# A hybrid transformer block: value steps in pairs in TensorE's order of a group

## What is computed

```python
x = x + _L0_attn_a_ref(_layernorm(x, axis=-1), L0_attn_a_w_qkv, L0_attn_a_w_o)
x = x + _L0_ffn_ref(_layernorm(x, axis=-1), L0_ffn_kernel, L0_ffn_scale)
x = x + _L0_attn_b_ref(_layernorm(x, axis=-1), L0_attn_b_w_qkv, L0_attn_b_w_o)
x = x + _L0_ffn_ref(_layernorm(x, axis=-1), L0_ffn_kernel, L0_ffn_scale)
```

```python
scores = jnp.einsum('bhsd,bhtd->bhst', xq, keys) * scale
causal = jnp.tril(jnp.ones((seq, seq), dtype=bool))[None, None]
scores = jnp.where(causal, scores, -jnp.inf)
probs = jax.nn.softmax(scores, axis=-1)
out = jnp.einsum('bhst,bhtd->bhsd', probs, values)
```

## Time and profile before

| | |
|---|---|
| runs, us | 1556.15, 1555.02, 1553.38 (median 1555.02) |
| span of the profiled execution, us | 1552.2 |
| busy: TensorE, VectorE, ScalarE, GpSimd | 1439.5, 1132.0, 998.2, 413.6 us |
| idle before the exponentials (L793), waiting for scores (L571) | 261.0 us |
| idle before the reductions (L974), waiting for L551 | 186.7 us |
| idle before the matmuls of L571, L549, L589 | 10.5, 17.9, 6.3 us |

### The profile page before, as it was taken

How to read it: one execution, slowest core, us unless ns; L and a number is a source line. 1 busy time by engine, 2 the same in 40 slices (tenths; PEclk the granted TensorE clock), 3 DMA queues, 4 the chain that set the end, 5 groups by cost and what they waited for, 6 DMA issues and landing times.

```text
span 1552.2 us, 36760 instructions
## 1 busy us (share of the span) xinstructions
PE 1439.5 (93%) x10756; PEld 799.7 (52%) x10756; DVE 1132.0 (73%) x1620; ACT 998.2 (64%) x1800; POOL 413.6 (27%) x786
## 2 busy tenths in 40 slices
PE   5989999998798999999879899999988899999997
PEld 4844444446674444444667444444466744444455
DVE  6897777736788777773768877777377887777646
ACT  4967667663496667675349667766625966776652
POOL 3423222212242322221224222222123422222211
PEclk9999999999899999999989999999998999999999
DMA  3000000001000000000210000000010000000001
GB/s 112 2 29 3 1 1 1 1 1 42 3 1 29 2 1 1 1 1 1 83 69 1 29 3 1 1 1 1 2 41 3 1 30 2 1 1 1 1 21 75
DMA packets 11421, 23.26 MB, mean 15 GB/s; under 512 B 816, under 2 KB 2608, under 8 KB 11312
## 3 DMA queue, kind: packets, MB, share of 16 engines
q1 hardware_dynamic: 11312, 21.89, 4.0%
HBM read 16.91 MB, written 4.19 MB: 14 GB/s over the span
## 4 chain that ended last, share of the span: by engine, by line
PE 73%; DVE 11%; issue 8%; POOL 3%; ACT 3%; DMA 1%; DVEq 0%; POOLq 0%; ACTq 0%; SPq 0%
PE psE L571 17%; PE psO L589 17%; PE psM L549 14%; PE psM L483 13%; DVE mx L974 4%; PE psM L551 3%; PE psT L466 2%; PE psT L532 2%; PE psO L532 2%; ACT probs L793 1%; PE psT L559 1%; DVE stats L876 1%; PE psE L466 1%; PE psM L466 1%; DVE xn L896 1%
## 5 line engine op out<-in xcount | busy, mean ns | idle before, releaser
L974 DVE TENSOR_REDUCE mx<-psM 128x1 f32<-128x768 f32 (+6 forms) x704 | 697.2, 1023 | 189.7 <-PE psM L551 186.7
L793 ACT ACTIVATE probs<-psE 128x512 f32<-128x512 f32 (+1 forms) x1216 | 656.8, 574 | 272.3 <-PE psE L571 261.0
L571 PE MATMUL psE<-qT,kT 115*128 (+4 forms) x1536 | 415.7, 331 | 10.5 <-ACT probs L793 7.4
L549 PE MATMUL psM<-kT,qT 112*128 (+4 forms) x1536 | 376.4, 327 | 17.9 <-DVE mx L974 13.8
L1163 POOL TENSOR_SCALAR_AFFINE_SELECT probs<-probs 128x512 f32<-128x512 f32 x256 | 162.3, 636 | 660.7 <-ACT probs L793 659.9
L589 PE MATMUL psO<-probs,v_grp 128*32 128x512 f32 (+3 forms) x3072 | 323.0, 499 | 6.3 <-POOL probs L1163 3.8
L571 PEld LDWEIGHTS psE<-qT,kT 115*128 (+1 forms) x1536 | 126.2, 97 | 289.0 <-ACT probs L793 152.5
L551 PE MATMUL psM<-tri_b,ident_b 128*128 128x128 bf16 x1024 | 210.3, 220 | 0.0
L549 PEld LDWEIGHTS psM<-kT,qT 112*128 (+1 forms) x1536 | 139.4, 98 | 108.6 <-DVE mx L974 31.1
L551 PEld LDWEIGHTS psM<-tri_b,ident_b 128*128 128x128 bf16 x1024 | 99.7, 97 | 65.5 <-issue 0.6
L589 PEld LDWEIGHTS psO<-probs,v_grp 128*32 128x32 f32 x3072 | 63.3, 108 | 104.3 <-issue 66.7
(11 more groups left out here) (90 smaller groups left out, 1553.8 us busy)
## 6 DMA issues: line engine op xcount, KB each, us to landing
probs<-in_w_qkv SPq DMA_DIRECT2D x5, 1536.0 KB, 6.3
xs<-in_x SPq DMA_DIRECT2D x8, 512.0 KB, 3.8
attn<-in_w_o SPq DMA_DIRECT2D x4, 1024.0 KB, 5.0
out_x<-xs SPq DMA_DIRECT2D x8, 512.0 KB, 3.0
qT<-nm_rows SPq DMA_DIRECT2D x64, 12.0 KB
probs<-in_w_ffn SPq DMA_DIRECT2D x1, 256.0 KB, 8.1
cos_s<-in_cos SPq DMA_DIRECT2D x1, 128.0 KB, 8.1
sin_s<-in_sin SPq DMA_DIRECT2D x1, 128.0 KB, 8.0
```

The source lines that it names most:

```text
L549: ins = pe.matmul(banks[:, at + k0:at + k1], qT[0:MAXROW, g * REP + h, qt * P:(qt + 1) * P], kT[0:MAXROW, g, k0:k1], start=True, stop=not ...
L571: ins = pe.matmul(psE[:, n % 2, at * w:(at + 1) * w], kT[0:DEPTH, g, kb * P:(kb + 1) * P], qT[0:DEPTH, g * REP + j, q0:q0 + w], start=True ...
L793: act.activation(probs[:, s % PSLOTS, heads[0]:heads[0] + len(heads), 0:w], psE[:, n % 2, 0:w * len(heads)].rearrange("p (h q) -> p h q", ...
L974: dve.tensor_reduce(mx[:, qt, heads[0]:heads[0] + len(heads)], src, AX.X, ALU.max).then_inc(unit_used.sem, 1)
```

## The change

Only the text `GROUP_ORDER` changes. The same items stand in it. The value steps stand in pairs (0 and 1, 2 and 3, and so on; 10 and 11 were a pair before), and the units and score items between them close up or move. The order of the S, of the U, of the N and O items among themselves stays.

```diff
--- before.py
+++ after.py
@@ -144,17 +144,17 @@
 
 GROUP_ORDER = """
 S.0.0 S.0.1 U.0 U.1 S.0.2 S.0.3 U.2
-S.1.0 N.1.0 S.1.1 U.3 S.1.2 U.4 S.1.3 PV.0
-S.2.0 U.5 S.2.1 U.6
-S.3.0 PV.1
-S.4.0 O.1.-1 S.4.1 U.7 S.4.2 U.8 S.4.3 PV.2
-S.5.0 U.9 S.5.1 U.10 S.5.2 PV.3 S.5.3 U.11
-S.6.0 U.12 S.6.1 PV.4 S.6.2 S.6.3 U.13 N.0.1 U.14
-S.7.0 S.7.1 PV.5 S.7.2 S.7.3 U.15 U.16
-S.8.0 S.8.1 PV.6 S.8.2 S.8.3 U.17 U.18
-S.9.0 S.9.1 PV.7
-S.10.0 PV.8 S.10.1 S.10.2 U.19 U.20 S.10.3
-S.11.0 PV.9 O.0.0 U.21 PV.10 PV.11
+S.1.0 N.1.0 S.1.1 U.3 S.1.2 U.4 S.1.3 U.5
+S.2.0 S.2.1 U.6 PV.0 PV.1
+S.3.0
+S.4.0 O.1.-1 S.4.1 U.7 S.4.2 U.8 S.4.3 PV.2 PV.3
+S.5.0 U.9 S.5.1 U.10 S.5.2 U.11 S.5.3
+S.6.0 U.12 S.6.1 U.13 S.6.2 S.6.3 PV.4 PV.5 N.0.1 U.14
+S.7.0 S.7.1 U.15 S.7.2 S.7.3 U.16
+S.8.0 S.8.1 U.17 S.8.2 S.8.3 PV.6 PV.7 U.18
+S.9.0 S.9.1
+S.10.0 U.19 S.10.1 S.10.2 U.20 S.10.3 PV.8 PV.9
+S.11.0 O.0.0 U.21 PV.10 PV.11
 """
 
 
```

## The result

The changed kernel takes 1620.35 us (median of 4 runs, 1617.49 to 1623.34) against 1555.59 for the kernel before; the ratio is 1.0423, 95% interval 1.0404 to 1.0442. Forecast were 1612 us and a range of 1586 to 1640. The span of the profiled execution went from 1552.2 to 1620.1 us.

A forecast was written before the change was run, and what follows sets the result against it. TensorE was taken to set the pace. Per group 3.79 us of waits less 1.15 (joins) and 0.66 (old small waits) gave 1.98; 24 x 1.98 + 4 x 2.4 = 57 us, so 1612 us, range 1586 to 1640.

The forecast's parts named there:

- The price of a join: Five new value-step pairs per group: each join saves 0.14 us inside and one 0.09 entry, 0.23; 1.15 us per group.
- the walk: New order followed item by item with trace durations: U.21 starts at 287.00 instead of 285.02, 1.98 us later per group.
- the signs: Expected profile: period about 32.85 us, TensorE busy time not higher, 512-column pairs 1.9 us, S.10.0 0.85 behind S.9.1.
- The drain rule: A change of tiling mode drains TensorE; by that rule alone the change gains 28 x 1.15 = 32 us.
- The waits: TensorE's score items and units between pairs wait for ScalarE and VectorE, two banks each: 3.79 us per group.
- The turn of the loop: From U.21 to the next group: nothing changes, PV.11's mask ready by 288.2, PV.11 starts at 288.5; no extra time.
- The first groups: First group of each round has 1.66 us more ScalarE work; 2.4 us extra each, between 2.0 and 2.9.
- Last groups as before: Sign: last groups of the rounds and all projections stay as before.
- the joins pay: Rival: only the drain counts, new waits stay under 1.8 us a group; 1505 us, joins alone 1523; chance 0.08.
- the two cancel: Rival: waits of 1.8 us a group offset the joins, no change, 1552 to 1558 us; chance 0.03.
- Restart costs compound: Rival: each wait also empties the sequencer's lead, 4.1 us a group, 115 us, 1670 us; chance 0.12.
- The clock gave way: Rival: granted clock falls because TensorE now idles; no size of its own, put inside the compounding-restart rival, chance 0.12.

The follow-up runs named there:

- triple_end: Kernel before with PV.9 moved behind U.21, to PV.10 and PV.11: 1550.99 us against 1554.34, ratio 0.9979.
- after_light: Changed kernel with exponentials over half their columns and reductions of maxima over half their keys: 1504.76 us, ratio 0.9679 to the kernel before.
- after_spread: Changed kernel, all pairs kept, U.18 moved between S.9.0 and S.9.1, U.19 ahead of step 10, U.20 behind S.10.1: 1608.27 us, ratio 1.0355 to kernel before.
- after_mask11: Changed kernel with GpSimd's mask of step 11 over one head of four: 1606.32 us, ratio 1.0326 to the kernel before.
- after_end_back: Changed kernel with the old order from step 8 on, pairs 6/7 and 8/9 undone: 1593.29 us, ratio 1.0251 to the kernel before.
- before_mask11: Kernel before with GpSimd's mask of step 11 over one head of four: 1552.81 us, ratio 0.9991.
- pair23: Kernel before with one join, PV.3 moved up to PV.2, S.5.3 then ahead of U.11: 1554.03 us against 1554.17, ratio 1.0002.
- n_later: Kernel before with N.0.1 moved behind S.7.0: 1548.49 us against 1555.76, ratio 0.9953.
- n_later_triple: Kernel before with both N.0.1 moved behind S.7.0 and PV.9 moved behind U.21: 1543.68 us against 1554.34, ratio 0.9938.

## Why the prediction was right

**The price of a join** (1.15 us a group) held where it can be read. PV.0 with PV.1 and PV.4 with PV.5 in the changed kernel, each with what starts behind it:

```profile
274.71 1.71 PE L589 MATMUL psO<-probs,v_grp 128*32 128x512 f32 x16
276.36 0.61 PE L571 MATMUL psE<-qT,kT 115*128 x5
...
284.77 1.92 PE L589 MATMUL psO<-probs,v_grp 128*32 128x512 f32 x16
286.51 0.39 PE L559 MATMUL psT<-ident_b,nm_parts 128*12 128x128 bf16 x4
```

PV.0 and PV.1 take 1.65 us instead of 1.00 + 0.79 (PV.1 alone before, 263.76 to 264.55): the 0.14 of the prediction, and the pairs 2/3, 6/7 and 8/9 give the same. PV.4 and PV.5 take 1.74 instead of 2.00, where the walk has 1.85 and the signs 1.9; behind them stand the transposes of N.0.1, and whether these are the reason was not tried. As a gain of the whole change the joins were never to be seen, as forecast. The drain rule of the Trainium skill, "TensorEngine Tiling (Array Packing)", section Key Properties, agrees in direction with these pairs and with triple_end, and would have given the wrong sign for the change.

**The waits** (3.79 us a group) were right in place and size. Walked and measured extra time, in us: U.5 0.42 and 0.41, S.4.1 0.29 and 0.28, U.11 0.34 and 0.34, S.6.3 0.27 and 0.27, S.10.0 0.63 and 0.64 (1.08 less two items of 0.22). Over the whole walked stretch +1.98 was said and +1.82 measured; PV.4 and PV.5 are 0.11 of the difference. after_light shows that the waits hang on the other engines' durations, after_spread that they hang on the items' places and not on the pairs.

**The turn of the loop** is the step that failed, inside a forecast that held: "Behind U.21 nothing changes, and the value steps' own inputs are there". The inputs were there for the matmul of PV.11 (300.10, the mask ended at 299.79) but not for its weight load, which before stood 0.46 us behind PV.10's. The branch and the register instructions of the next group came only once the mask was done: the branch follows the mask's end by 0.16 us in the changed kernel and in after_mask11. It cost 0.62 us in the steady group and 0.55 in the mean of the 24 groups of the loop, of which after_mask11 took 0.34 back and after_end_back all. The walk put nothing down for S.11.0's move behind PV.9: S.11.0 now starts 1.26 us ahead of PV.10 instead of 2.17, and with it its exponential and its mask. That this move alone is the cause was not tried; after_end_back also undoes two pairs.

**The first groups** were given 2.4 us each. In the windows of round 0 it is 34.25 - 31.70 = 2.55, over the four rounds 2.43.

**The sum.** 57 us were forecast and 64.8 measured (67.9 between the two spans). From the first exponential of group 0 to that of group 7, summed over the rounds, it is 867.7 us before and 934.2 after: the 28 groups give 66.5. The 24 groups of the loop give 2.37 each, 1.82 in the walked stretch (forecast 1.98) and 0.55 in the turn (forecast 0); the four first ones 2.43 (forecast 2.4). So the walk was 4 us too high and the turn, 13 us, was missing: that the forecast came within 8 us is owed in part to an error that went the other way. "Last groups as before" held for the work but not for the time: the clock fell in all four, before in two, 2.8 us in all. What is left, 1.4 us less, lies outside the groups.

**The rivals.** That the joins pay, or that the two cancel, is refuted for this order. "Restart costs compound" (4.1 us a group) did not happen: the period rose by 2.44. Its kernel of truth is the turn, where the instructions of the next group come late. The clock gave way in the last groups, see below.

## What to carry to other kernels

A long item on the bound engine is cover for the engines that feed on its shorter items; put two together and, with two banks between them, the second one covers nothing. Before changing an order, walk one period item by item with starts, durations and bank rules from the trace: here this gave the place of each of the larger waits and its size to 0.05 us. For every wait that "is met in time", check the weight load and not the matmul, and what stands behind it in the queue, above all a loop's branch. And before a few us of a total are put down to an edit, sum the periods that the edit touches.

## What was not expected of the hardware

The granted clock fell at the start of the last groups, in some of them. The changed kernel's last group in the first round took 39.04 us at a mean of 0.96, before 37.70 at 1.00. The stretch is at half, the lower of the two levels (1.2 GHz):

```profile
337.10:340.50 3.40, 3.40 (x18) 1.05 (x15) 0.41 (x1) 1.29 (x4) 0.27 (x1) 0.50 0.01 4
```

In the kernel before, the same happened in the second round:

```profile
701.32:740.41 39.09, 36.45 (x218) 18.30 (x218) 13.88 (x33) 24.10 (x50) 5.78 (x13) 0.96 0.01 2
```

and in after_mask11 the first round's last group is at 1.00:

```profile
333.56:371.49 37.93, 35.20 (x218) 17.82 (x218) 14.06 (x34) 24.05 (x50) 5.88 (x14) 1.00 0.01 2
```

A last group with such a stretch takes 38.4 to 38.5 us from its first exponential to its last, one without it 37.0 to 37.1, in all the traces with whole exponentials: 1.4 us each. The work is the same, and the stretch begins 2.4 to 3.4 us after the first exponential. What each trace shows, summed over its four rounds:

| kernel | 28 periods, us | last groups with a fall, of 4 |
|---|---|---|
| before | 867.7 | 2 |
| before_mask11 | 867.7 | 3 |
| pair23 | 868.2 | 3 |
| triple_end | 865.2 | 0 |
| n_later | 864.2 | 0 |
| n_later_triple | 861.7 | 0 |
| the changed kernel | 934.2 | 4 |
| after_mask11 | 926.9 | 0 |
| after_spread | 923.1 | 0 |
| after_end_back | 909.8 | 1 |

Ahead of the fall TensorE waits for ScalarE's exponentials (a gap of 1.24 us of weight loads at 335.04 in the changed kernel), but the same gap stands in the last group of the earlier trace rows, where the clock did not fall. A late turn does not explain it either: after_spread has it and none of the four fell. What decides it stays open; each trace is one execution. It costs up to 5.6 us of a total, as much as the smaller effects of this study.
